# Layer two's norm and convolution inside its attention program, query blocks in the order 2, 3, 1, 0, and the opening work of both attention stages dealt between the row maxima

## The reference, cut to what matters

```python
# a0: all keys
q = q * cos + _rotate_half(q) * sin
k = k * cos + _rotate_half(k) * sin
attn = softmax((q @ k.T) * 8 ** -0.5)           # 16 heads of 8 columns, 2048 x 2048
out = (attn @ v) @ wo.T + bo
# ... experts, then an attention with 8 heads of 128 columns ...
# a1: causal
h = _layernorm(x, ln1_w, ln1_b)
h = conv(h, conv_w)                             # h[t] = w0*h[t-2] + w1*h[t-1] + w2*h[t], each column by itself
q, k, v = split(h @ attn_w)                     # rotated as above
p = softmax(where(causal, q @ k.T / sqrt(8), -1e30))
x = x + (p @ v) @ proj_w
# then x = x + the output of one of four experts per token, and a last norm
```

## Time and profile before

| what | us |
|---|---|
| median of 3 runs (lowest, highest) | 2094.41 (2093.96, 2098.53) |
| the profiled execution | 2091.26 |
| its span in the trace | 2089.2 |
| a0, opening: from the first product of L491 to the first score of L578 | 6.57 to 102.87 |
| a0, main loop | 102.87 to some 740 |
| `norm_conv` | 1496.15 to 1506.07 |
| a1, opening | 1506.59 to 1594.53 |
| a1, main loop: from the first score to the last copy of L693 | 1594.53 to 1971.24 |

### The profile page before, as it was taken

How to read it: one execution, slowest core, us unless ns; L and a number is a source line. 1 busy time by engine, 2 the same in 40 slices (tenths; PEclk the granted TensorE clock), 3 DMA queues, 4 the chain that set the end, 5 groups by cost and what they waited for, 6 DMA issues and landing times. The chain is left out here.

```text
span 2089.2 us, 40754 instructions
## 1 busy us (share of the span) xinstructions
PE 1853.3 (89%) x16072; PEld 929.9 (45%) x16072; DVE 1550.8 (74%) x2264; ACT 1382.2 (66%) x2565; POOL 365.2 (17%) x522
## 2 busy tenths in 40 slices
PE   6799999999999686748998999999778999999785
PEld 2122222222223286714676776767612333334385
DVE  6899999999996332435787677787578989876434
ACT  3499999999998332325554556666346898888431
POOL 4201000000002322142442122121241000000213
PEclk8699999999999798869999999999877999999798
DMA  5000000000000367500000000000100000000174
GB/s 167 1 3 4 5 9 4 9 5 5 10 7 4 115 219 225 180 20 0 1 1 1 1 1 1 1 1 1 53 0 1 4 5 11 5 12 6 49 262 155
DMA packets 53021, 81.70 MB, mean 39 GB/s; under 512 B 9216, under 2 KB 37888, under 8 KB 52704
## 3 DMA queue, kind: packets, MB, share of 16 engines
q1 hardware_dynamic: 47664, 70.63, 10.8%
q0 software_dynamic: 3072, 6.30, 1.0%
q10 hardware_dynamic: 2096, 2.17, 0.4%
HBM read 64.26 MB, written 12.06 MB: 37 GB/s over the span
## 5 line engine op out<-in xcount | busy, mean ns | idle before, releaser
L787 DVE TENSOR_REDUCE a_mx<-psum 128x2 f32<-128x1024 f32 (+2 forms) x832 | 907.4, 1160 | 79.7 <-PE psum L559 42.6
L713 ACT ACTIVATE a_cs<-psum 128x512 f32<-128x512 f32 (+3 forms) x1664 | 858.3, 571 | 95.4 <-PE psum L528 35.7
L603 PE MATMUL psum<-a_cs,a_V 128*16 128x256 f32 (+1 forms) x6400 | 503.6, 386 | 12.7 <-ACT a_OD L693 8.8
L559 PE MATMUL psum<-a_KS,a_QS 48*128 48x512 bf16 (+3 forms) x1664 | 328.5, 385 | 31.4 <-DVE a_mx L787 28.5
L578 PE MATMUL psum<-a_QS,a_KS 51*128 51x512 bf16 (+3 forms) x1664 | 340.8, 379 | 15.4 <-issue 7.5
L2083 PE MATMUL psum<-b_VW,b_ST 128*128 128x129 f32 x2176 | 252.6, 277 | 12.9 <-DVE X L2193 12.9
L2083 PEld LDWEIGHTS psum<-b_VW,b_ST 128*128 128x128 f32 x2176 | 248.6, 194 | 14.6 <-DVE X L2193 14.6
L578 PEld LDWEIGHTS psum<-a_QS,a_KS 51*128 51x128 bf16 x1664 | 88.5, 93 | 367.2 <-ACT a_cs L713 315.8
L2064 PE MATMUL psum<-b_GT,AT 128*128 128x512 f32 (+3 forms) x640 | 243.1, 534 | 1.6 <-ACT b_ST L2119 1.6
L603 PEld LDWEIGHTS psum<-a_cs,a_V 128*16 128x16 f32 x6400 | 107.3, 94 | 232.0 <-issue 121.0
L2168 DVE TENSOR_TENSOR b_M<-b_M,b_ST 128x512 f32<-128x512 f32 (+3 forms) x288 | 174.9, 607 | 42.6 <-ACT b_ST L2119 12.8
(11 more groups left out here) (227 smaller groups left out, 1536.8 us busy)
## 6 DMA issues: line engine op xcount, KB each, us to landing
e_W<-in_l_experts SPq DMA_DIRECT2D x45, 576.0 KB
e_W<-in_l_experts SPq DMA_DIRECT2D x21, 768.0 KB, 5.9
yg<-e_yout SPq DMA_DIRECT2D x14, 256.0 KB
xg<-zeros SPq DMA_DIRECT2D x2, 1472.0 KB, 9.5
a_cs<-in_rope ACTq DMA_DIRECT2D x4, 512.0 KB, 9.9
a_QS<-a_mrow SPq DMA_DIRECT2D x128, 3.0 KB
a_cs<-in_rope SPq DMA_DIRECT2D x1, 2048.0 KB, 7.9
a_num<-a_OD SPq DMA_DIRECT2D x120, 16.0 KB
```

Of the source, the lines that this page charges most:

```text
L559: mm = pe.matmul(ps[:, 2 * slot + half, 0:width], QS[rows, 2 * p + i, q_cols(qb, qt * P, P)], KS[rows, 2 * p + i, c * BLK:c * BLK + width] ...
L603: mm = pe.matmul(ps[32 * j:32 * j + 2 * HD, AV_BANK, a:b], V[:, kt, HPP * p + j, :], probs(e, a, b), start=(kt == 0 and half == 0), stop=last,
L713: act.activation(probs(HPP * s + j, c, BLK), ps[:, plan.bank(entry), c:BLK], ACT.Exp, scale=scale).then_inc(exp_done, 1)
L787: dve.tensor_reduce(mx[:, pk % 2, qt, 2 * i:2 * i + 2, c], banks, AX.X, ALU.max).then_inc(max_done, 1)
```

## The change

In both attention stages:

- From operand 4 on (`WHOLE`), a projection is cut into two halves of 256 columns, each with a ring slot of its own and a `turn` of its own (`parts`, `turned`).
- `lead_order` writes the row of an operand as one list: half projections, single terms of the placing rounds (`place_term`, four products), and behind each such token one maximum, while there are any.
- POOL splits the maxima of pack 0 (`maxima(0)`) between its work on two operands and no longer behind all of it; in a0 POOL also casts the four mask tables (`cast_masks`), which stood on DVE behind operand 1.

In layer two alone:

- `norm_conv` becomes the class `Convolution`, and its work is written into the attention's program: DVE convolves blocks 0 and 2, norms block 3, and goes on with operand 0 before it convolves block 1; block 3 is convolved behind operand 0's placing. V of block 3 moves to row 3, into a ring slot.
- Query blocks run 2, 3, 1, 0. Pack 0 then has 24 maxima over three key blocks (rows 2 to 4), `beyond` is 21, and rows 5 to 7 have 7 each with the turn of pack 0 in row 5. In the main loop the maxima per pack of the first eight packs, 32, 32, 29, 27 (16 steps each) and 24, 24, 20, 20 (12 steps each) before, are now 16, 24, 27, 29 (12 steps each) and 32, 32, 27, 21 (16 steps each); where 27 and 29 stand, eight half-steps have two. The last eight packs are as before.
- The rotation tables come as four DMAs of 512 KB and not as one of 2 MB.

The diff, cut to its core:

```diff
@@ Plan
-        self.ring = [("project", s, j) for s in range(2) for j in range(2)]
-        for s, mine in enumerate(self.lead):
-            if s + 2 < len(self.operands):
-                self.ring += [("project", s + 2, 0)] + mine[:1] + [("project", s + 2, 1)] + mine[1:]
-            else:
-                self.ring += mine
+        self.opened = [("project", s, j, 0) for s in range(2) for j in range(2)]
+        self.order_of_lead = [self.lead_order(s, mine) for s, mine in enumerate(self.lead)]
+        self.ring = self.opened + [item for row in self.order_of_lead for item in row if item[0] != "set"]
...
-        half = (len(left) + 1) // 2
-        lead[2 + NB] += left[:half]
-        lead[3 + NB] += left[half:]
+        open_ = range(2 + self.chunks(self.order[0]), len(lead))
+        each = -(-(len(left) - 1) // len(open_))
+        left.remove(("turn", 0))
+        for n, s in enumerate(open_):
+            lead[s] += left[n * each:(n + 1) * each]
+        lead[open_[0]].insert(TURN_AFTER, ("turn", 0))
+    def lead_order(self, s, mine):
+        ahead = [("project", s + 2, j, h) for j in range(2) for h in range(self.parts(s + 2))] if s + 2 < len(self.operands) else []
+        first, second = ([("set", v, t) for t in range(TERMS)] for v in range(2))
+        if s == 0:
+            return ahead + first + second
+        if s == 1:
+            return first + ahead[:1] + second + ahead[1:]
+        out, left = [], list(mine)
+        def deal(group):
+            for token in group:
+                out.append(token)
+                if left:
+                    out.append(left.pop(0))
+        deal(ahead[:len(ahead) // 2])
+        deal(first)
+        deal(ahead[len(ahead) // 2:] + ([("values", NB - 1)] if self.causal and s == LATE_VALUES else []))
+        deal(second)
+        return out + left
@@ small_head_stage, GpSimd
+                if conv:
+                    conv.norm.begin(pool)
+                    pool.memset(V[:, :, :, HD:], 1.0).then_inc(consts_set, 1)
+                    conv.norm.power(pool, 0, conv.LATE)
...
+                for s in range(NOP):
+                    split_rest(s)
+                    if s == 3 + plan.chunks(order[0]):
+                        maxima(0)
+                    if s + 1 < NOP:
+                        rotate(s + 1)
+                    split_low(s)
+                    if opening and s == NB:
+                        opening.cast_masks(pool)
@@ TensorE
-                def place_set(s, v):
+                def place_term(s, v, t):
...
+                if conv:
+                    project(0, 0, 0)
+                    project(0, 1, 0)
+                    values(V_ORDER[0])
+                    project(1, 0, 0)
+                    project(1, 1, 0)
+                    conv.norm.transpose(pe, 0, conv.BANK)
+                    for g in V_ORDER[1:V_FIRST]:
+                        values(g)
@@ ScalarE
+                    if conv and s == 0:
+                        conv.late_rows(act)
+                    if conv and s == 2:
+                        conv.norm.keep(act, 0, conv.LATE)
@@ VectorE
+                if conv:
+                    conv.begin(dve)
+                    conv.norm.variance(dve, conv.chain, conv.LATE)
+                    conv.taps(dve, conv.SEQUENCE[0])
+                    conv.taps(dve, conv.SEQUENCE[1])
+                    conv.norm.normalize(dve, 0, conv.LATE)
+                for j in range(2):
+                    turn(0, j, 0)
+                if conv:
+                    conv.taps(dve, conv.SEQUENCE[2])
...
+                    if conv and s == 0:
+                        conv.taps(dve, conv.LATE)
+class Convolution:
+    SEQUENCE = (0, 2, 1, 3)
+    def late_rows(self, act):
+        self.norm.store(act, 0, self.LATE, self.BANK)
+        act.wait_ge(self.norm.h_ready, 1)
+        self.tap(act, self.LATE)
@@ two_layers
+        forward, causal_order = list(range(NB)), [2, 3, 1, 0]
-                           [x[0:n * P, :] for x, n in zip(xg, slots)], (d1.table_in, 16), forward[::-1], 2, a["l1_experts"], 4, wide)
+                           [x[0:n * P, :] for x, n in zip(xg, slots)], (d1.table_in, 16), causal_order, 2, a["l1_experts"], 4, wide)
```

More of the change, by code:

```diff
@@ L242, in small_head_stage @@
 def small_head_stage(core, tag, src_T, w, bias, cs, arrived, KS, QS, V, place, kbias, OT, causal, order, beyond,
-                     tokens, opening, later, front):
+                     tokens, opening, later, front, conv):
     nc, ps = core.nc, core.psum
@@ L257, in small_head_stage @@
     MAXIMA = len(plan.items)
+    V_ORDER = list(conv.SEQUENCE if conv else range(NB))
+    V_FIRST = NB - 1 if conv else NB
     SELF = P - HPP * HD
@@ L436, in _, with maxima @@
                 rotate(0)
-                pool.memset(V[:, :, :, HD:], 1.0).then_inc(consts_set, 1)
+                if not conv:
+                    pool.memset(V[:, :, :, HD:], 1.0).then_inc(consts_set, 1)
                 if opening:
                     pool.memset(opening.zeros[:, :], 0.0).then_inc(opening.zeroed, 1)
-                for s in range(NOP):
-                    split_rest(s)
-                    if s + 1 < NOP:
-                        rotate(s + 1)
-                    split_low(s)
-                pool.wait_ge(consts_set, 3)
-                for pk in range(NPK):
+                def maxima(pk):
                     u = pk % 2
@@ L459, in _ @@
                     pool.wait_ge(split_done, pk + 1)
+                for s in range(NOP):
[7 more added lines that the diff above has]
+                        opening.cast_masks(pool)
+                pool.wait_ge(consts_set, 3)
+                for pk in range(NPK):
+                    if pk:
+                        maxima(pk)
                     if pk == NPK - 1:
@@ L697, in _ @@
                     act.wait_ge(*arrived["bias"])
+                if conv:
+                    for g in conv.SEQUENCE[:-1]:
+                        conv.tap(act, g)
                 split_high(0)
@@ L843, in _ @@
                             invert(k)
+                if conv:
+                    dve.wait_ge(conv.norm.kept, TPB)
                 front.vector_early(dve)
@@ new lines, with __init__, sync, begin @@
+class Convolution:
+    SEQUENCE = (0, 2, 1, 3)
+    LATE = 3
+    BANK = 1
+    def __init__(self, core, st, tag, X, cT, hpad, gamma, beta, cw, early):
+        sem = lambda n: core.sem(st, f"{tag}_{n}")
+        self.cT, self.hpad, self.cw, self.early = cT, hpad, cw, early
+        self.norm = BlockNorm(core, st, tag, X, hpad, 1, gamma, beta)
+        self.tap_ready, self.ready = sem("tap_ready"), sem("ready")
+        self.chain = Chain(None, sem("chain"))
+        self.arrived = [(self.ready, self.SEQUENCE.index(g) + 1) for g in range(NB)]
+    def sync(self, sp):
+        for dst, src, arrived in self.early:
+            sp.dma_start(dst, src).then_inc(arrived, 16)
+    def begin(self, dve):
+        self.chain.eng = dve
+    def tap(self, act, g):
+        act.activation(self.cT[:, g * BLK:(g + 1) * BLK], self.hpad[:, g * BLK:(g + 1) * BLK], ACT.Copy,
+                       scale=self.cw[:, 0:1]).then_inc(self.tap_ready, 1)
+    def late_rows(self, act):
+        self.norm.store(act, 0, self.LATE, self.BANK)
+        act.wait_ge(self.norm.h_ready, 1)
+        self.tap(act, self.LATE)
+    def taps(self, dve, g):
+        dve.wait_ge(self.tap_ready, self.SEQUENCE.index(g) + 1)
+        mine = self.cT[:, g * BLK:(g + 1) * BLK]
+        for k in (1, 2):
+            ins = dve.scalar_tensor_tensor(out=mine, in0=self.hpad[:, g * BLK + k:(g + 1) * BLK + k],
+                                           scalar=self.cw[:, k:k + 1], in1=mine, op0=ALU.mult, op1=ALU.add)
+            if k == 1:
+                self.chain.link(ins)
+                self.chain.settle()
+        ins.then_inc(self.ready, 1)
```

230 lines of the change are left out of this document (98 added, 132 removed).

## The result

The changed kernel takes 2102.93 us (median of ten runs, 2093.53 to 2109.64), the kernel before 2094.61 on the same chip: ratio 1.0031, interval 1.0016 to 1.0047. By the ratio it is slower by 6.5 us, by the two medians by 8.3, where I forecast 7 less. Its profiled execution took 2104.76, span 2102.5, against 2091.26 and 2089.2.

What follows compares the result with a forecast made beforehand. In the openings no engine was full, DVE and PE taking turns; main loops had nothing idle. Terms -6.6 -1.9 +5.0 -4.5 -1.3 +5 -3 gave -7.3 us, 2084.0 profiled, 2087 as median; range 2074 to 2098.

Steps and rivals of the forecast that it cites:

- Row 1: a0's opening up to row 2: casts moved from DVE to POOL and operand 1's earlier round save 1.9 us.
- Rows 2 to 5: a0's opening: dealt pieces shrink DVE's idle 3.38 us a row, rows take 11.9 us; four rows save 6.6 us.
- PE at 1.2 GHz bounds the openings: Rival for both openings: TensorE at its low clock sets the rows, total -0.8 us, 2093.6 us; chance 0.18.
- a1's loop: a1's main loop: third and fourth packs with 27 and 29 maxima cost 5 us, the first pack saves 3.
- Rows 6 and 7: End of a0's opening: single terms wait for ACT's copies, 21.4 us at 1.2 GHz; costs 5.0 us.
- The head of layer two: Layer two's start to row 2: PE starts earlier amid the merged norm and convolution; saves 4.5 us.
- Rows 2 to 7 of a1: a1's opening, row 2 to first score: 63.8 us instead of 65.1, saving 1.3 us.
- The slower rival, placing rounds as the bound in rows 2 to 5,: Every one of eight rows waits for at least one pair of ACT's copies: +17 us, 2104 us; chance 0.12.
- the signs that I had named: Trace signs of being right: a0 rows near 12 us, first scores earlier in a0 by 3 to 4, a1 6 to 7.

Runs made afterwards that it cites:

- Number 1: Changed kernel with row 1 of both openings in the old order, both projections of operand 3 ahead of operand 1's rounds: 1.0030 times the kernel before.
- number 7: Changed kernel with old row 1, a1's first four packs at 24 maxima each, spaced whole rounds in rows 6 and 7: 0.9948 times the kernel before.
- number 8: Changed kernel without the dealing: merged convolution and new block order kept, openings in old order with whole projections and rounds: 1.0015 times the kernel before.
- number 9: The kernel of number 7 with whole projections in all rows: 2076.78 us against 2095.29, 0.9913 times the kernel before.
- number 10: The kernel of number 8 with a1's first four packs at 24 maxima each: 0.9970 times the kernel before.
- number 2: Changed kernel with rows 6 and 7 of both openings in the old order, whole rounds; rows 2 to 5 stay dealt: 1.0009 times the kernel before.
- number 6: Changed kernel with whole projections of 512 columns in all rows, single terms still dealt between maxima: 1.0009 times the kernel before.
- number 5: Changed kernel run again unaltered, on another chip beside the kernel before: 1.0057 times the kernel before.
- Number 4: Changed kernel with the dealt openings alone: separate norm and convolution block, block order 3, 2, 1, 0, one rotation-table DMA: 1.0062 times the kernel before.
- Number 3: Changed kernel with the maxima of a1's first four packs spread evenly, 24 each: 1.0021 times the kernel before.

## Why the prediction was wrong

- **Row 1 (forecast -1.9, measured +2.5).** The first failed step. I counted the earlier round of operand 1 as a gain and didn't follow the two projections that it pushed back: turn, POOL's addition, the low term behind it, the next turn. What stood there instead is a wait of 2.58 us for the low term, in both stages. Number 1 takes 4.8 us out of a0's opening. With the old order of row 1 (numbers 1, 7, 8, 9 and 10) row 2 starts 24.4 to 25.9 us after the first product, where the kernel before had 26.2; so the casts gave 0.4 to 1.8 of the 1.9, and the order of row 1 is nearly the whole miss.
- **Rows 2 to 5 (forecast -6.6, measured -3.7).** The price of PE's pieces was mis-sized. I halved and divided the times of whole groups; a half costs 1.16 and not 1.03, a term 0.55 and not 0.46. Why a piece costs more than its share is not shown. With these the floor at 1.2 GHz was 12.3 a row. I also took 11.9, between the two clocks; the clock fell from 0.67 to 0.57. The rival "PE at 1.2 GHz bounds the openings" had -4.2, +5.5 and +2.3 for a0's rows, its end and a1's rows; measured are -3.7, +5.6 and +1.8. For the openings it was the right case, though row 3 shows that it isn't the whole of it; with the misses of row 1 (4.4) and of a1's loop (3.3) added, its 2093.6 becomes 2101.3, against 2102.93.
- **Rows 6 and 7 (forecast +5.0, measured +5.6).** Right in size and mechanism (the waits that I listed for the range's end come to 5.7 and not 5.5); numbers 2 and 7 show that the end of row 5 is part of it. What I missed is that the halves cause part of it, ten pieces for eight maxima: without them 2.6 of the 5.6 are gone (number 6).
- **The head of layer two (forecast -4.5, measured -3.7).** Right in the main, with luck in the size: the early start of PE gives more, and the late turn of row 1, which I hadn't seen, takes 2.6 of it. Run again (number 5) the stretch took 30.9 and not 29.6. The taps took 2.41 for two where they had taken 1.53.
- **Rows 2 to 7 of a1 (forecast -1.3, measured +1.8).** Run again (number 5) it took 68.3 and not 66.9, +3.2. Number 4, set against the trace of the kernel before, has dealing losing 1.7 in the row of short maxima and 6.6 at the end. That these are the same prices of PE and the same bare terms as in a0 is argued from a0 and not tested by itself.
- **a1's loop (forecast +5 and -3, measured +6.7 and -1.7).** The doubled half-steps came as I described, inside the range given; the first pack was 3.6 us longer than the second and not some 2 (its clock was 0.87, and 0.88 in the kernel before). Number 3 gives all of the first term back.
- **The slower rival, placing rounds as the bound in rows 2 to 5,** was not what happened: no wait for copies stands there. The time came out near its 2104 by chance, as a sum of smaller things. With row 1, the rows of both stages and the loop as measured the forecast of -7.3 would have been +6.4, against +8.3 between the medians.

Of the signs that I had named, the rows of a0 near 12 us, the short turns (0.48 and 0.42), the rounds released by ACT's copies and the packs over 28 us came. The two first scores did not: a0's came 4.3 us later, counted from its first product, and a1's 1.8 earlier, counted from the start of its layer, and not 6 to 7.

What stays open: 5.6 us of the difference of the two profiled executions lie where the instructions are the same. The stretch from the end of a0's loop to layer two took 755 to 763 us in the eight executions on chips of the 2050 kind, with no order in it. What the rotation tables as four DMAs give was not run by itself, nor was number 7 beside number 9.

## What to carry to other kernels

When work is cut into smaller pieces for an engine, price a piece from start to start at the clock that the stretch has, and count pieces against what is to be dealt between them: pieces left over gather at the end of the row, where the next round waits for their copies. When one operation is moved forward, follow what it pushes back through every in-order queue to the buffer that the next row reuses. And when blocks are reordered, lay the due work evenly: eight half-steps with two maxima, in two packs, cost 7 to 8 us here, and an even spread nothing.

## What the runs showed of the hardware

TensorE's clock did not rise with denser work: rows 2 to 5 of a0 ran at 0.67 in 54.2 us before and at 0.57 in 50.5 after; without the dealing (number 8) they ran at 0.61 in 54.5, and with it in numbers 6 and 9 at 0.65 and 0.58 in 49.1 and 49.6. PE's busy share (0.70 before, 0.90 after) is no measure of the work, as it holds the lower clock already.

VectorE and GpSimd held each other up (seen in every kernel with the merging, not tested by itself). A tap of VectorE took 0.75 in the kernel before, where GpSimd was idle beside the last six. Beside GpSimd's addition of operand 0 (L467, 1512.56 to 1514.27) the first tap took 0.74 and the second, from 1513.18, 1.64, and the addition 1.70 where the next two took 1.28 and 1.27. The Trainium skill, page "SBUF — State Buffer", section "SBUF: two separate sides", has the two engines share a pair of ports that one of them locks for a whole instruction, where VectorE reads two inputs from SBUF; the trace agrees: the addition is longer by 0.4 when 0.6 of the first tap was left at its start, and the second tap by 0.9 when 1.1 of the addition was left.

Two kinds of chip showed. In the last 20 us of a0's loop ACT, in the changed kernel of the first comparison, stood idle three times for 3 to 5 us with a releaser that the profile calls remote. The same kernel on the other kind of chip had no such wait; its a0 loop was 15 us shorter, all of it in the last pack (37 us and not 53), and the middle stretch 29. What the two kinds differ in is not shown:

```profile
703.48 1.32 ACT L782 ACTIVATE a_cs<-psum 128x512 f32<-128x512 f32 x2 [5.28 <-remote]
```
